# A gated cross-attention block on one core: value products in two visits of six tiles instead of three of four, and the work around them re-timed

## The chip, the cores and the metric

The kernel runs on one core of a Trainium2 chip. The metric is the device time of one execution in microseconds (us). Three executions of the kernel before took 1373.48, 1373.49 and 1373.64 us; the median is 1373.49 us.

## The reference

For 32 batches, a layer norm of x (100 x 256) attends with 16 heads of 16 channels to a context of 1444 tokens, and a gated feed-forward part with quantized weights follows. Shortened:

```
x (32, 100, 256); ctx (32, 1444, 256); mask (32, 1444)
q = layernorm(x) @ Wq.T + bq;  k = ctx @ Wk.T + bk;  v = ctx @ Wv.T + bv      # 16 heads x 16
probs = softmax(clip(where(mask, clip(q k^T / 4, -50, 50), -10000), -50, 50))
delta = clip(residual_scale, 0, 0.3) * ((probs @ v) @ Wo.T + bo)
x = x + tanh(g_xattn) * (layernorm(delta) * gamma + beta)
n = activation_quant(layernorm(x))                       # 127 / max|row|, rounded
h = silu(n @ weight_quant(w1).T) * (n @ weight_quant(w2).T)      # hidden 704
x = x + tanh(g_ffn) * (activation_quant(h) @ weight_quant(w3).T)
```

## The kernel before

All matmuls run transposed: tokens of the context lie on partitions. The 1444 tokens of a batch are 12 tiles of 121 (the last has 113), and three chunks of four tiles. A batch `b` is a loop of 12 steps `n = 0..11`, and each engine has its own written-out program of these steps; only semaphores tie the programs together. `c` is the next batch, `d` the one before.

In step n TensorE (PE) does, in this order: `scores(b, n, 0)` (L1196: four matmuls for one half of the head pairs), half of a context item, a piece of a neighbour batch's small work, the value products if the step has them ("a visit"), `scores(b, n, 1)`, and the other half of the context item. ScalarE (ACT) takes each score half through an exponential into one of `NE` buffers `e_sb`, VectorE (DVE) clips the whole tile (`clip`, L787, 121 x 1600), and a visit (`attend`, `pv`, L1216) multiplies `VISIT` clipped tiles with the values into one PSUM bank; each tile waits for its own clip, and is 32 matmul records. In the kernel before the visits are in steps 1, 5 and 9, over the four tiles up to n - LAG = n - 2.

A context item `w` of 12 makes keys or values: chunk u = w // 4 has two key items (L1237, 484 columns each) and two value items (L1251). Item w runs in step w + ITEM, so with ITEM = 4 the items 8 to 11 of a batch run in steps 0 to 3 of that batch itself, the others in steps 4 to 11 of the batch before. Around an item: `split_head` and `split_rest` (DVE, L748 and L754, in steps 1/2, 5, 9) turn a loaded chunk into a high and a low part, and `split_head` of a chunk must wait until the last value item of the chunk two before it (`pe_ctx`) has read the same buffer; `k_rest` (DVE, L778) makes the low part of the keys.

Then SP issues the stacking: `stack_k` is 12 DMAs (L305) that lay a chunk's keys into one of two `k_st` buffers, after the keys are there and after the second score half of the last tile of the chunk that held the buffer. The stack of c's chunk 0 waits for `scores(b, 7, 1)` and is awaited by `scores(c, 0, 0)`; chunk 1 runs from step 11 to step 4, chunk 2 from step 3 to step 8. `stack_q` is 12 DMAs issued by GpSimd (POOL, L476) for the queries, in its step 8, after `q_rest` (DVE, L833, step 6).

The small work: attention output of d (DVE `attention_read` L848 in step 1, `attention_out` step 2; PE `delta` L1284 in step 3; DVE `delta_out` L873 in step 3), x of d for the feed-forward (DVE step 5), `x_turn` L1268, `x_query` L1275 (PE steps 4 and 5), `x2_turn` L1290 (7), gate and up products `up` L1302 (8 to 10), then `h_max`, `h_scale`, `h_round`, `h_quant` on DVE, `h_turn` L1309 (PE, step 1 of the batch after) and `down` L1315 (step 2). `x_turn` waits for `delta_out`. A second, guarded pass over all batches exists in the program (the branches with `base`) and runs only if non-finite values were seen.

## Time and profile before

| | us |
|---|---|
| median of three executions | 1373.49 |
| the profiled execution | 1372.54 |
| its span, first to last instruction | 1370.8 |
| PE busy / DVE busy / ACT busy / POOL busy | 1310.4 / 1124.0 / 961.6 / 457.0 |
| one batch in the middle (613.33 to 653.33) | 40.0 |

The span has a set-up of some 55 us in which the weights are prepared, 32 batches, and a tail from about 1335 us in which the last batch's small work runs alone. A busy share is an average over all of these. Matmuls overlap, so the distance from one start to the next is what one costs, and the printed duration of a single one is longer than that.

### The profile page before, as it was taken

What the parts mean: (1) busy time and instruction counts of PE and PEld (TensorE: products, weight loads), DVE (VectorE), ACT (ScalarE), POOL (GpSimd) and SP (SyncE); (2) the same over time, 40 slices, a digit from 0 to 9 for tenths busy, and PEclk for the clock granted to TensorE, in tenths of its full rate; (3) what the DMA queues carried; (4) which work ended last, traced back from release to release, by engine and by line L of the source; (5) the groups of instructions that cost most, each with busy time, mean ns of one, the idle gap of its engine ahead of it and who ended that gap; (6) DMA issues with size and microseconds to landing.
All of it is one profiled execution on the core that took longest, in us unless ns stands there. A gap on an engine that the chain in (4) does not pass through costs nothing.

```text
span 1370.8 us, 48003 instructions
## 1 busy us (share of the span) xinstructions
PE 1310.4 (96%) x19984; PEld 1211.7 (88%) x19984; DVE 1124.0 (82%) x2241; ACT 961.6 (70%) x1602; POOL 457.0 (33%) x760
## 2 busy tenths in 40 slices
PE   5599999999999999999999999999999999999982
PEld 4599999999999999999999999999999999999971
DVE  5668888888888888888888888888888888888864
ACT  2367777777777777777777777777777777777761
POOL 3623332333332233333223333423333332333310
PEclk9699999999999999999999999999999999999995
DMA  7467667767776776776677677767777776777620
GB/s 213 104 164 175 166 162 170 174 161 184 175 163 160 176 165 161 187 178 161 165 179 170 157 191 170 167 161 168 167 170 184 168 167 166 171 171 168 152 62 8
DMA packets 142477, 222.12 MB, mean 162 GB/s; under 512 B 29162, under 2 KB 135598, under 8 KB 142254
## 3 DMA queue, kind: packets, MB, share of 16 engines
q1 hardware_dynamic: 129966, 199.31, 60.5%
q0 software_dynamic: 12288, 19.69, 6.7%
q8 instruction: 159, 2.61, 0.9%
q14 instruction: 64, 0.52, 0.1%
HBM read 54.00 MB, written 3.28 MB: 42 GB/s over the span
## 4 chain that ended last, share of the span: by engine, by line
PE 87%; SPq 4%; DVE 3%; DMA 2%; POOL 2%; ACT 1%; issue 1%; DVEq 0%; POOLq 0%; ACTq 0%
PE sc L1196 22%; PE pvb L1216 19%; PE cb L1251 18%; PE cb L1237 17%; SPq L305 4%; PE mb L1302 3%; PE mb L1275 2%; PE mb L1284 2%; DMA k_st<-k_lo 2%; PE mb L1315 2%; PE mb L1309 1%; POOL q_st L476 0%; PE mb L1268 0%; ACT e_sb L554 0%; POOL e_sb L514 0%
## 5 line engine op out<-in xcount | busy, mean ns | idle before, releaser
L554 ACT ACTIVATE e_sb<-sc 121x800 f32<-121x800 f32 (+1 forms) x768 | 645.9, 847 | 150.9 <-PE sc L1196 138.5
L1196 PE MATMUL sc<-q_st,k_st 96*121 96x200 f32 (+1 forms) x3072 | 476.2, 278 | 9.5 <-DMA q_st<-bd_hi 4.1
L1196 PEld LDWEIGHTS sc<-q_st,k_st 96*121 96x121 f32 (+1 forms) x3072 | 415.1, 187 | 38.2 <-issue 10.9
L787 DVE TENSOR_SCALAR e_sb<-e_sb,hi_b 121x1600 f32<-121x1600 f32 (+1 forms) x384 | 400.2, 1049 | 5.9 <-ACT e_sb L554 5.9
L1216 PE MATMUL pvb<-e_sb,v_sb 121*32 121x100 f32 x12288 | 286.4, 251 | 0.0
L1216 PEld LDWEIGHTS pvb<-e_sb,v_sb 121*32 121x32 f32 x12288 | 265.1, 110 | 22.3 <-issue 19.2
L1251 PE MATMUL cb<-wv_hi,c_hi 128*121 128x256 f32 (+1 forms) x768 | 222.3, 289 | 9.9 <-DVE k_lo L778 9.7
L778 DVE SCALAR_TENSOR_TENSOR k_lo<-cb,bk_c,k_hi 128x484 fp32r<-128x484 f32 (+1 forms) x192 | 134.4, 701 | 110.5 <-ACT k_hi L566 110.5
L1251 PE MATMUL cb<-wv_hi,c_lo 128*121 128x256 f32 (+1 forms) x768 | 216.3, 282 | 0.0
L1251 PE MATMUL cb<-wv_lo,c_hi 128*121 128x256 f32 (+1 forms) x768 | 216.2, 282 | 0.0
L476 POOL DMA_DIRECT2D q_st<-bd_hi x256 | 164.6, 647 | 115.9 <-DVE bd_lo L833 113.1
L447 POOL TENSOR_SCALAR d_ve<-dmv,scal 100x1 f32<-100x1 f32 x32 | 43.9, 1373 | 433.4 <-DVE dmv L883 433.4
L1237 PE MATMUL cb<-c_hi,wk_hi 128*128 128x484 f32 (+1 forms) x384 | 154.5, 402 | 0.0
L1251 PEld LDWEIGHTS cb<-wv_hi,c_hi 128*121 128x121 f32 (+1 forms) x768 | 142.2, 185 | 11.2 <-DVE k_lo L778 10.4
L1237 PE MATMUL cb<-c_lo,wk_hi 128*128 128x484 f32 (+1 forms) x384 | 147.1, 383 | 0.0
L1237 PE MATMUL cb<-c_hi,wk_lo 128*128 128x484 f32 (+1 forms) x384 | 147.1, 383 | 0.0
L1251 PEld LDWEIGHTS cb<-wv_hi,c_lo 128*121 128x121 f32 (+1 forms) x768 | 141.3, 184 | 0.1
L1251 PEld LDWEIGHTS cb<-wv_lo,c_hi 128*121 128x121 f32 (+1 forms) x768 | 140.4, 183 | 0.0
L566 ACT ACTIVATE k_hi<-cb,bk_c 128x484 fp32r<-128x484 f32 (+1 forms) x192 | 127.4, 664 | 4.8 <-PE cb L1237 4.8
L754 DVE TENSOR_TENSOR c_lo<-c_in,c_hi 128x968 fp32r<-128x968 f32 (+1 forms) x96 | 112.5, 1172 | 0.0
L575 ACT ACTIVATE v_sb<-cb 121x512 f32<-121x512 f32 x160 | 97.1, 607 | 21.0 <-PE cb L1251 21.0
L476 POOL DMA_DIRECT2D q_st<-bd_lo x128 | 91.3, 713 | 0.1
(139 smaller groups left out, 1529.5 us busy)
## 6 DMA issues: line engine op xcount, KB each, us to landing
k_st<-k_hi SPq DMA_DIRECT2D x512, 121.0 KB, 2.8
c_in<-in_ctxT SPq DMA_DIRECT2D x64, 484.0 KB, 3.9
k_st<-k_lo SPq DMA_DIRECT2D x256, 121.0 KB, 3.0
k_st<-k_hi SPq DMA_DIRECT2D x256, 119.0 KB, 3.4
c_in<-in_ctxT SPq DMA_DIRECT2D x32, 476.0 KB, 4.7
k_st<-k_lo SPq DMA_DIRECT2D x128, 119.0 KB, 3.1
q_st<-bd_hi POOLq DMA_DIRECT2D x256, 50.0 KB, 3.3
q_st<-bd_lo POOLq DMA_DIRECT2D x128, 50.0 KB, 3.3
```

Source lines behind the costliest of these rows:

```text
L305: sp.dma_start(k_st[st_slot(b, u)][QR * part:QR * (part + 1), :, j, 0:CL[u]].bitcast(f32), src[slot][QR * j:QR * (j + 1), :, 0:CL[u]].bitc ...
L476: nc.gpsimd.dma_start(q_st[b.par][QR * part:QR * (part + 1), :, j, :].bitcast(f32), src[QR * j:QR * (j + 1), :, :, :].rearrange("p k a s - ...
L554: nc.scalar.activation(e_sb[e_slot(b, n)][0:TL[n], k * SW:(k + 1) * SW].rearrange("p (o c) -> p o c", o=2), sc[q % NSC][0:TL[n], :, 0:2 * PW],
L566: nc.scalar.activation(k_hi[slot][:, o, 0:CL[u]], cb[o][:, 0:CL[u]], ACT.Identity, bias=bk_c[:, o:o + 1]).then_inc(k_hi_done, 1)
L575: nc.scalar.activation(v_sb[0:TL[n], n:n + 2, :, 0:4:3, :].rearrange("p n q a d -> p (n q) a d"), cb[i][0:TL[n], :].rearrange("p (q a d) - ...
L754: V.tensor_tensor(c_lo[slot][:, :, 0:w], c_in[slot][:, :, 0:w], c_hi[slot][:, :, 0:w].bitcast(f32), ALU.subtract).then_inc(split_done, 1)
L778: V.scalar_tensor_tensor(k_lo[slot][:, o, 0:w], cb[o][:, 0:w], bk_c[:, o:o + 1], k_hi[slot][:, o, 0:w].bitcast(f32), ALU.add, ALU.subtract ...
L787: V.tensor_scalar(e, e, E_LO, hi_b[b.par][0:TL[n], n:n + 1], ALU.max, ALU.min).then_inc(clip_done, 1)
L1196: last = T_.matmul(sc[q % NSC][0:TL[n], e // 2, (e % 2) * PW:(e % 2 + 1) * PW], k_st[st_slot(b, n // TPC)][:, pr // NQ, pr % NQ, t0:t0 + T ...
L1216: last = T_.matmul(pvb[QR * j:QR * (j + 1), col:col + S], v_sb[0:TL[n], n, pr, 2 * a:2 * a + 2, :].rearrange("p x d -> p (x d)"), e[0:TL[n ...
L1237: last = T_.matmul(cb[o][:, 0:w], wt[:, k, o * P:(o + 1) * P], ct[slot][:, k, 0:w], start=i == 0, stop=i == 5)
L1251: last = T_.matmul(cb[i][0:TL[n], half * H:(half + 1) * H], ct[slot][:, k, t0:t0 + TL[n]], wt[:, k, :], start=(k == 0 and a == 0), stop=(k ...
```

## The change

`VISIT` goes from 4 to 6 and `LAG` from 2 to 1: the visits are in steps 0 (tiles 6 to 11 of d) and 6 (tiles 0 to 5 of b). `NE` goes from 6 to 7 exponential buffers; the room comes from the guard's scratch tiles, which now lie in the seventh buffer (the guarded pass uses six), and two memsets of them leave the set-up. `ITEM` goes from 4 to 5: every context item, with its ACT and DVE parts, is one step later. The four gate and up products stand one each in PE steps 8, 9, 10 and 11, all ahead of the second score half; the ACT and DVE parts follow, so that `hidden_up(d, 1)` and `h_max` move from DVE's steps 10 and 11 into step 0 of the next batch.

```diff
-    NE = 6
-    VISIT = 4
+    NE = 7
+    NEG = 6
+    VISIT = 6
-    LAG = 2
-    ITEM = 4
+    LAG = 1
+    ITEM = 5
...
+        care = [e_sb[NE - 1][:, i * H:(i + 1) * H] for i in range(6)]
...
         def e_slot(b, n):
-            return (NT * b.par + n) % NE
+            return (NT * b.par + n) % NEG if b.base else (NT * b.n + n) % NE
...
-            nc.gpsimd.memset(big_pos[:, :], INF_TO)
-            nc.gpsimd.memset(big_neg[:, :], -INF_TO)
...
-                    if prev and n in (9, 10):
-                        ffn_up(d, n - 9)
-                    if prev and n in (8, 9):
-                        ffn_gate(d, n - 8)
+                    if prev and n in (8, 10):
+                        ffn_gate(d, (n - 8) // 2)
+                    if prev and n in (9, 11):
+                        ffn_up(d, (n - 8) // 2)
...
-                        if n in (9, 10):
-                            hidden_gate(d, n - 9)
+                        if n in (9, 11):
+                            hidden_gate(d, (n - 9) // 2)
...
                     if prev2 and n == 0:
-                        for step in (h_scale, h_round, h_quant):
+                        hidden_up(b.plus(-2), 1)
+                        for step in (h_max, h_scale, h_round, h_quant):
                             step(b.plus(-2))
...
-                        if n in (9, 10):
-                            hidden_up(d, n - 9)
-                        if n == 11:
-                            h_max(d)
+                        if n == 10:
+                            hidden_up(d, 0)
...
-                    has_pv = n % VISIT == 1 and (n > VISIT or prev)
+                    has_pv = n % VISIT == 0 and (n >= VISIT or prev)
...
-                        if n == 8:
-                            up(d, 0, 0)
-                        if n in (9, 10):
-                            up(d, n - 9, 1)
+                        if n >= 8:
+                            up(d, (n - 8) // 2, n % 2)
                     attend()
                     if prev2 and n == 1:
                         h_turn(b.plus(-2))
-                    if prev and n == 9:
-                        up(d, 1, 0)
```

How the instructions stand in three places. The first is VectorE in steps 0 and 1 of a steady batch, from the clip of the last tile (113 partitions) to the first read of the attention sums (`oT<-pvb`). Before:

```order
L787 TENSOR_SCALAR e_sb<-e_sb,hi_b 113x1600 [waits exp_done]
L943 TENSOR_SCALAR tiny<-tiny 100x1 [waits dve_post]
L945 RECIPROCAL tiny<-tiny 100x1 [waits dve_post]
L949 TENSOR_SCALAR th<-gs,tiny 100x704 [waits dve_post]
L953 TENSOR_SCALAR hq<-th 100x704 [waits dve_post]
L954 TENSOR_SCALAR tiny<-tiny,k_y 100x1
L748 CAST c_hi<-c_in 128x968 [waits pe_ctx,c_loaded1]
L778 SCALAR_TENSOR_TENSOR k_lo,watch<-cb,bk_c,k_hi 128x476 [waits k_hi_done]
L787 TENSOR_SCALAR e_sb<-e_sb,hi_b 121x1600 [waits pool_x,exp_done]
L848 TENSOR_SCALAR oT<-pvb,submask 128x200 [waits pv_done]
```
After:

```order
L788 TENSOR_SCALAR e_sb<-e_sb,hi_b 113x1600 [waits exp_done]
L936 TENSOR_TENSOR gs<-th,us 100x352 [waits dve_post,act_post]
L940 TENSOR_REDUCE tiny<-gs 100x1 [waits dve_post]
L944 TENSOR_SCALAR tiny<-tiny 100x1 [waits dve_post]
L946 RECIPROCAL tiny<-tiny 100x1 [waits dve_post]
L950 TENSOR_SCALAR th<-gs,tiny 100x704 [waits dve_post]
L954 TENSOR_SCALAR hq<-th 100x704 [waits dve_post]
L955 TENSOR_SCALAR tiny<-tiny,k_y 100x1
L749 CAST c_hi<-c_in 128x968 [waits pe_ctx,c_loaded1]
L788 TENSOR_SCALAR e_sb<-e_sb,hi_b 121x1600 [waits pool_x,exp_done]
L849 TENSOR_SCALAR oT<-pvb,submask 128x200 [waits pv_done]
```
Behind the clip stand two more operations (`gs`, the reduce to `tiny`); the key part `k_lo` that stood between the cast of the next chunk (`c_hi<-c_in`, chunk 0 of c) and the clip has gone to a later step. The cast waits for `pe_ctx`: it needs item 7 of the batch, which before ran in step 11 of the batch ahead and now runs in step 0, its second half behind the visit.

The second place is TensorE in steps 5 and 6, from the query product (`mb<-xnT,wq`) on. Before, the visit follows it at once:

```order
L1275 MATMUL mb<-xnT,wq 128x100 [waits act_x]
L1275 MATMUL mb<-xnT,wq 128x100 x3
L1216 MATMUL pvb<-e_sb,v_sb 32x100 [waits dve_post,v_done,clip_done]
L1216 MATMUL pvb<-e_sb,v_sb 32x100 x15
L1216 MATMUL pvb<-e_sb,v_sb 32x100 [waits clip_done]
L1216 MATMUL pvb<-e_sb,v_sb 32x100 x15
```
After, from the same product's second row on, the visit (`pvb`) comes one step later, in step 6, behind two score halves and two key halves (`cb`):

```order
L1277 MATMUL mb<-xnT,wq 128x100 x3
L1198 MATMUL sc<-q_st,k_st 121x200 [waits exp_done]
L1198 MATMUL sc<-q_st,k_st 121x200 x3
L1239 MATMUL cb<-c_hi,wk_hi 128x484
L1239 MATMUL cb<-c_lo,wk_hi 128x484
L1239 MATMUL cb<-c_hi,wk_lo 128x484
L1198 MATMUL sc<-q_st,k_st 121x200 [waits exp_done]
L1198 MATMUL sc<-q_st,k_st 121x200 x3
L1239 MATMUL cb<-c_hi,wk_hi 128x484 [waits v_done]
L1239 MATMUL cb<-c_lo,wk_hi 128x484
L1239 MATMUL cb<-c_hi,wk_lo 128x484
L1218 MATMUL pvb<-e_sb,v_sb 32x100 [waits dve_post,v_done,clip_done]
```
It now takes tiles 0 to 5, and the sixth of them waits for the clip that VectorE does in this same step 6.

The third place is TensorE in step 9, between the score half that frees a stacking buffer (step 7) and the one that needs it (step 0 of the next batch). Before:

```order
L1237 MATMUL cb<-c_hi,wk_hi 128x484 [waits v_done]
L1237 MATMUL cb<-c_lo,wk_hi 128x484
L1237 MATMUL cb<-c_hi,wk_lo 128x484
L1302 MATMUL mb<-w12q,x2T 100x352 [waits act_post]
L1302 MATMUL mb<-w12q,x2T 100x352
L1216 MATMUL pvb<-e_sb,v_sb 32x100 [waits v_done,clip_done]
L1216 MATMUL pvb<-e_sb,v_sb 32x100 x15
L1216 MATMUL pvb<-e_sb,v_sb 32x100 [waits clip_done]
L1216 MATMUL pvb<-e_sb,v_sb 32x100 x15
L1216 MATMUL pvb<-e_sb,v_sb 32x100 [waits v_done,clip_done]
```
After:

```order
L1239 MATMUL cb<-c_hi,wk_hi 128x484 [waits v_done]
L1239 MATMUL cb<-c_lo,wk_hi 128x484
L1239 MATMUL cb<-c_hi,wk_lo 128x484
L1304 MATMUL mb<-w12q,x2T 100x352 [waits act_post]
L1304 MATMUL mb<-w12q,x2T 100x352
L1198 MATMUL sc<-q_st,k_st 121x200 [waits exp_done]
L1198 MATMUL sc<-q_st,k_st 121x200 x3
L1239 MATMUL cb<-c_hi,wk_hi 128x484
L1239 MATMUL cb<-c_lo,wk_hi 128x484
L1239 MATMUL cb<-c_hi,wk_lo 128x484
```
The visit that stood here, four tiles, is gone; no value product is left between steps 7 and 0.

## Rows read from the trace of the kernel before

**Rows 1.** The page: busy time by engine, and TensorE clock in 40 slices.
```profile
PE 1310.4 (96%) x19984; PEld 1211.7 (88%) x19984; DVE 1124.0 (82%) x2241; ACT 961.6 (70%) x1602; POOL 457.0 (33%) x760
...
PEclk9699999999999999999999999999999999999995
```

**Rows 2.** TensorE waits of the whole span: engine line waited for, total, times, longest.
```profile
PE sc L1196 <- DMA k_st<-k_lo: 2.0, 6, 0.7
```

**Rows 3.** TensorE timeline: start, us, instruction, shapes, count.
```profile
603.79 0.46 PE L1302 MATMUL mb<-w12q,x2T 128*100 128x352 bf16 x2
604.18 2.97 PE L1216 MATMUL pvb<-e_sb,v_sb 121*32 121x100 f32 x128
607.08 0.50 PE L1302 MATMUL mb<-w12q,x2T 128*100 128x352 bf16 x2
...
619.55 0.44 PE L1309 MATMUL mb<-identb,hq 100*128 100x100 bf16 x6
...
631.44 2.96 PE L1216 MATMUL pvb<-e_sb,v_sb 121*32 121x100 f32 x128
...
639.04 0.65 PE L1196 MATMUL sc<-q_st,k_st 96*121 96x200 f32 x4
...
653.33 0.47 PE L1196 MATMUL sc<-q_st,k_st 96*121 96x200 f32 x3
```

**Rows 4.** Chain of waits, same stretch: start, us, and what ran.
```profile
607.58 0.41 PE sc L1196 x4
607.99 0.68 PE cb L1237 x3
```

**Rows 5.** VectorE timeline, same batch.
```profile
613.61 0.88 DVE L939 TENSOR_REDUCE tiny<-gs 100x1 f32<-100x704 f32 x1
...
616.93 0.66 DVE L748 CAST c_hi<-c_in 128x968 fp32r<-128x968 f32 x1
...
619.69 0.42 DVE L848 TENSOR_SCALAR oT<-pvb,submask 128x200 f32<-128x200 f32 x1 [0.50 <-PE pvb L1216]
...
631.01 0.48 DVE L893 SCALAR_TENSOR_TENSOR x<-dn,d_r,x_res 100x256 f32<-100x256 f32 x1 [1.07 <-POOL d_r L452]
...
638.27 1.05 DVE L787 TENSOR_SCALAR e_sb<-e_sb,hi_b 121x1600 f32<-121x1600 f32 x1
639.23 0.57 DVE L833 SCALAR_TENSOR_TENSOR bd_lo<-bd,bd_hi 128x400 fp32r<-128x400 f32 x1
...
647.84 0.53 DVE L935 TENSOR_TENSOR gs<-th,us 100x352 f32<-100x352 f32 x1
```

**Rows 6.** Issues of the stacking copies: timelines of the SP queue and of GpSimd.
```profile
627.31 1.23 SPq L305 DMA_DIRECT2D k_st<-k_hi  x2
...
635.64 0.60 SPq L305 DMA_DIRECT2D k_st<-k_lo  x1
...
639.77 1.93 SPq L305 DMA_DIRECT2D k_st<-k_hi  x2
...
650.51 0.61 SPq L305 DMA_DIRECT2D k_st<-k_lo  x1
...
799.72 1.23 SPq L305 DMA_DIRECT2D k_st<-k_hi  x2
...
808.93 1.02 SPq L305 DMA_DIRECT2D k_st<-k_lo  x1
...
640.45 1.40 POOL L476 DMA_DIRECT2D q_st<-bd_hi  x1 [2.97 <-DVE bd_lo L833]
...
647.87 0.54 POOL L476 DMA_DIRECT2D q_st<-bd_hi  x1
```

**Rows 7.** Stretches of the last batch: width, busy PE to POOL, clock, DMA share, GB/s.
```profile
1318.00:1319.00 1.00, 0.34 (x5) 0.17 (x3) 1.00 (x2) 1.00 (x3) 1.00 (x1) 1.00 0.47 109
1320.00:1321.00 1.00, 1.00 (x7) 1.00 (x6) 0.39 (x1) 1.00 (x3) 0.00 (x0) 0.50 0.00 0
1322.00:1323.00 1.00, 1.00 (x22) 0.76 (x24) 0.90 (x1) 1.00 (x3) 0.00 (x0) 0.50 0.00 0
```

More of the change, by code:

```diff
@@ L101, in flamingo_block @@
     INF_TO = 10000.0
-    assert 2 * NT % NE == 0 and (STEPS * NT) % NSC == 0 and NB % 2 == 0 and NB >= 8
+    assert 2 * NT % NEG == 0 and NEG < NE and NT % VISIT == 0 and (STEPS * NT) % NSC == 0 and NB % 2 == 0 and NB >= 8
     assert all(c % 2 == 0 for c in CL) and STEPS * SW == EW
@@ L137, in flamingo_block @@
         odd, odd_sum = sb("odd", [P, 1]), sb("odd_sum", [P, 1], i32)
-        big_pos, big_neg = sb("big_pos", [P, H]), sb("big_neg", [P, H])
-        g_pos, g_k = sb("g_pos", [P, H]), sb("g_k", [P, H])
-        g_gt, g_lt = sb("g_gt", [P, H], i32), sb("g_lt", [P, H], i32)
         x_in = [sb(f"x_in{i}", [S, H]) for i in range(2)]
@@ L162, in flamingo_block @@
         e_sb = [sb(f"e_sb{i}", [P, EW]) for i in range(NE)]
+        care = [e_sb[NE - 1][:, i * H:(i + 1) * H] for i in range(6)]
+        big_pos, big_neg, g_pos, g_k = care[0:4]
+        g_gt, g_lt = care[4].bitcast(i32), care[5].bitcast(i32)
         zt, oT = sb("zt", [P, KT, S]), sb("oT", [P, KT, S])
@@ L202, in flamingo_block @@
         stored = sem("stored")
-        odd_known = sem("odd_known")
+        odd_known, care_known = sem("odd_known"), sem("care_known")
         care_c, care_k, care_v = sem("care_c"), sem("care_k"), sem("care_v")
@@ L519, in passes @@
                 if base:
+                    nc.gpsimd.memset(big_pos, INF_TO)
+                    nc.gpsimd.memset(big_neg, -INF_TO).then_inc(care_known, 1)
                     x_rstd_of(whole(0, base))
@@ L552, in exps @@
                 if k == 0 and not (isinstance(b.n, int) and b.n == 0 and n < NE):
-                    act.wait_ge(pv_done, TILE.after(b, n) - NE)
+                    act.wait_ge(pv_done, TILE.after(b, n) - (NEG if b.base else NE))
                 nc.scalar.activation(e_sb[e_slot(b, n)][0:TL[n], k * SW:(k + 1) * SW].rearrange("p (o c) -> p o c", o=2),
@@ L1111, in passes @@
                 if base:
+                    dve.wait_ge(care_known, 1)
                     b = whole(0, base)
@@ L1142, in passes @@
                 clip(e, NT - 1)
-                for step in (h_scale, h_round, h_quant, result):
+                hidden_up(e.plus(-1), 1)
+                for step in (h_max, h_scale, h_round, h_quant, result):
                     step(e.plus(-1))
```

## The prediction

> **What bounds the kernel now.** I read the page first: TensorE is busy for 96% of the span, VectorE for 82%, ScalarE for 70%, and TensorE's clock is full but for the set-up and the tail [rows 1]. In the list of TensorE's waits nothing of the 32 batches matters; the one to remember is small, six waits of 2.0 us together, for the stacking DMAs of the keys [rows 2]. So a batch takes 40 us because TensorE has 40 us of matmuls, and no matmul goes away in this change. It can gain only at the borders between kinds of matmul, and lose by waits that are now just hidden. So I read TensorE's timeline of one batch for the distances [rows 3, 4], and VectorE's and SP's timelines of the same batch for how early the things that it needs are ready [rows 5, 6].
>
> **The visits themselves.** A visit of four tiles takes 2.90 us (604.18 to 607.08), 0.725 a tile [rows 3]; six tiles take 4.35. One visit less per batch saves its border: the gate product's two matmuls start 0.39 us before the visit [rows 3], some 0.2 more than two such matmuls need, and a score half behind a visit takes about 0.1 more than the 0.41 of rows 4. Against that, the gate and up products, of which two lay at a visit, now stand between a context half and a score half four times, at about 0.1 each. I count 0 (bounds -0.3 and +0.2 a batch).
>
> **First wait: the clip of tile 5, in step 6.** With LAG at 1, the visit in step 6 needs the clip that VectorE does in step 6; before, that clip was wanted only in step 9. What sets VectorE's time is a second edit: with ITEM at 5, the last value item of chunk 1 runs in step 0, its second half behind the visit, and the cast of the next chunk at the head of VectorE's step 1 waits for it. Before, that cast began at 616.93, 2.6 us before TensorE had finished its visit of step 1 (619.55) [rows 3, 5]. Now VectorE is through with step 0 early and then stands until step 0 of TensorE has ended; behind the cast are queued, in order, the clip of tile 0, the attention sums, the key parts, three clips and the whole chain to the feed-forward's input.
>
> From the end of TensorE's step 0, VectorE needs: the cast 0.66, a clip 0.96 (638.27 to 639.23), then everything from the attention read to the end of clip 5, 619.69 to 639.23 = 19.54 [rows 5]. Three key parts lie in that stretch in both kernels. Sum 21.2, and 0.14 for the hand-over (619.69 against 619.55) [rows 3, 5], at both ends: 21.4.
>
> TensorE needs, until it reaches tile 5: a score half and a key half, 0.41 + 0.68 [rows 4]; from the transposes of step 1 to the end of the query product 619.55 to 631.44 = 11.89 [rows 3]; then two score halves and two key halves, 2.2; about 0.1 to enter the visit; five tiles, 3.6. Sum 18.9. It waits 21.4 - 18.9 = 2.5; I take 2.4, since the cast overlaps the next operation a little. (A part of it will show earlier, at `x_turn` in step 4, which waits for `delta_out` of VectorE's step 3; that is the same lateness, not more.) Bounds: 1.3, if VectorE's pause of 1.07 for GpSimd inside the 19.54 [rows 5] vanishes; 3.1, if a key part has to wait for ScalarE. 30 batches of 2.4: 72 us.
>
> **Second wait: the stack of chunk 0, in step 0.** The 12 DMAs of the next batch's chunk 0 can start when `scores(b, 7, 1)` is done, and `scores(c, 0, 0)` wants them. Before, the distance on TensorE was 639.04 to 653.33 = 14.3 us, with the visit of step 9 in it [rows 3]. Without that visit it is 14.3 - 2.9 - 0.2 = 11.2. The other two chunks gain what this one loses, a visit now lies in each of their stretches and is longer.
> The stack needs: 0.73 until SP starts (639.77), then to the last issue 10.74 in this batch, 9.21 in another (799.72 to 808.93), and 8.33 for chunk 2 (627.31 to 635.64), when GpSimd issues nothing [rows 6]; then the landing, under 2.82, since TensorE went on at 653.33 without a wait [rows 3]. GpSimd's 12 query DMAs take 640.45 to 648.4 and began 0.7 us after the stack [rows 6]; now they begin some 2.5 before it, as they hang on step 6's clip, so about two thirds of them still lie beside it. I take 9.1 to the last issue and 2.7 to land: 0.73 + 9.1 + 2.7 = 12.5, a wait of 1.3. Bounds: 0.73 + 8.33 + 2.3 - 11.2, about 0.2 (the 2.3 is my estimate for a landing half a microsecond under its bound), and 0.73 + 10.74 + 2.82 - 11.2 = 3.1. I stay at the typical batch, as rows 2 show that the 10.74 is near the worst. 31 batch starts of 1.3: 40 us.
> The Trainium skill ("DMA: Bandwidth & Descriptors", Issuing engines are not separate DMA queues) says that DMAs issued by different engines run on the same 16 DMA engines and interleave. Rows 6 agree (10.74 beside GpSimd's, 8.33 without). By that rule alone the two thirds of an overlap would put the last issue at 9.9 and the wait at 2.2, 27 us more in all, inside the bounds.
>
> The two waits add up: the first delays `scores(b, 7, 1)`, from which the second is counted, and the second delays step 0, whose end starts VectorE's 21.4 us again.
>
> **TensorE's clock.** In the last batch, where TensorE had work for 0.34 of the microsecond 1318 to 1319, its clock was at half from 1320 on, and still at 1322 to 1323 [rows 7]. A wait of 1.5 to 2.4 us in one piece may do the same. Some 3 us at half speed cost 1.5; behind the step 6 wait half of it is swallowed by the second wait. I count it in every other batch: 30 x 0.4 = 12 us (bounds 0 and 45).
>
> **The rest.** `hidden_up` and `h_max` (0.53 and 0.88 [rows 5]) move into VectorE's step 0, where it stands idle for the cast anyway, so they are covered; `h_turn` in step 1 wants the result over 7 us after step 0 begins. In the tail they are bare, 1.4 us, and the last visit has two tiles more, 1.45: 3 us. Batch 0 has one context item less and the last batch one more: 0. The seventh buffer has no price: step 6's exponentials write it before the visit frees tile 0's. Without it ScalarE would stand. Two memsets fewer in a set-up that waits for weights: 0. In steps 8 to 11 ScalarE has no visit to catch up in; its two exponentials, an item and a gate stay just under TensorE's step, cover thin, and if gone, a few tenths a batch.
>
> Sum: 72 + 40 + 12 + 3 = 127 on the profiled execution's 1372.5 gives 1499.5; the median of the runs is 0.95 above that execution, so 1500 us.
>
> **Rivals.** (1) *Only the clip wait.* The stack of chunk 0 gets through in the shorter stretch, because the DMA load spreads over a longer batch. For it: 8.33 without GpSimd. Against: even then nothing is left over. 1373.5 + 72 + 12 + 3 = 1460.
> (2) *All at the upper bounds*, with the clock falling each time: 30 x 3.1 + 31 x 3.1 + 45 + 3 = 237, 1611 us. For it: rows 6's slow stack, rows 7. Against: only six small waits in the kernel before.
> (3) *Both waits about half as long*, since I mis-add the lateness of an engine that has 18% of idle time [rows 1]: 1373.5 + 60 = 1433.
> (4) *Faster.* VectorE is done with clip 5 in time and the stack lands in time; then a batch has one visit border less, 0.3 us, 31 times: 1364 us. It decides at 2.4 us on VectorE's path: if the cast of chunk 0 began where it did before, 2.6 us ahead of the visit's end, this case would hold. The waits of the code speak against it: the cast waits for the value item now in step 0.
> The Trainium skill ("TensorEngine Tiling (Array Packing)", Key Properties) says that changing the tiling mode drains the engine; the visits use another mode (32 output rows) than their neighbours. The 0.39 us before the visit agrees; by that rule the change gains this rival's 0.3 us per batch and nothing else.
>
> **Chances.** Forecast 0.57, with its own range 1455 to 1550; (1) 0.15; (2) 0.13, mostly its lower part, 1550 to 1611; (3) 0.10; (4) 0.05. Runs of this kernel tell apart about 0.2%, 2.7 us. Slower by over 0.2%: (1), (2), (3) and the forecast, 0.95; case (4) is split, within 0.2% 0.02 (the border of a visit worth nothing), faster 0.03. The range 1420 to 1565 holds the forecast, (1) and (3) and the foot of (2), about 0.83.
>
> **What the profile after would show.** The first wait: TensorE standing in front of the last 32 value matmuls of step 6's visit, waiting for VectorE's clip, or at `x_turn` for `delta_out`, together some 2.4 us a batch, and VectorE idle before the cast by about 2.5 us with `cb`'s value item as releaser. The second: TensorE's step 0 waiting for `k_st` by some 1.3 us, 31 times. A batch would take 43.6 to 44 us, and TensorE's clock would show slices under full. The forecast is wrong if VectorE is not idle before that cast, or if clip 5 ends before TensorE is through with tile 4, or if step 0 starts without a wait for the stack.

## The result and the profile after

| | kernel before | changed kernel |
|---|---|---|
| median of the runs | 1373.49 us (1371.28 to 1373.64, 4 runs) | 1491.47 us (1483.22 to 1494.61, 4 runs) |
| profiled execution, span | 1372.54 us, 1370.8 us | 1489.05 us, 1487.2 us |
| mean granted clock of TensorE | 0.975 | 0.964 |

The change makes the kernel slower: ratio 1.085, 95% interval 1.081 to 1.090. The profiled execution took 116.5 us more. Line numbers of the changed kernel differ from those before by one or two (the scores are L1198, the visits L1218, the value items L1253, the clip L788, the cast L749).

The page after, first the busy times, then the clock; it answers to [rows 1].

```profile
PE 1353.5 (91%) x19984; PEld 1235.1 (83%) x19984; DVE 1140.1 (77%) x2241; ACT 959.4 (65%) x1602; POOL 511.4 (34%) x758
...
PEclk9699999999999999999999999999999999999995
```

The instructions of TensorE are as many as before; its share fell from 96 to 91%. The 40 slices of the clock hide what a batch does, as will be seen. The chain of work that ended last, by engine, shows who took over: VectorE, with 3% of it before and 37% after. First the kernel before, then the changed one:

```profile
PE 87%; SPq 4%; DVE 3%; DMA 2%; POOL 2%; ACT 1%; issue 1%; DVEq 0%; POOLq 0%; ACTq 0%
```

```profile
PE 45%; DVE 37%; POOL 6%; issue 6%; SPq 3%; DMA 2%; ACT 1%; DVEq 0%; POOLq 0%; ACTq 0%
```
 The waits say more (engine and line, what it waited for, us in total, times, longest); it is the same view as [rows 2], in which six waits for `k_st` made 2.0 us.

```profile
PE pvb L1218 <- DVE e_sb L788: 50.7, 31, 2.2
...
PE mb L1270 <- DVE dl L874: 12.6, 30, 0.4
...
PE pvb L1218 <- issue: 7.2, 12, 1.1
...
PE sc L1198 <- DMA k_st<-k_lo: 4.2, 6, 1.2
```

The first two are new, and each comes about once a batch: the last 32 matmuls of step 6's visit wait for the clip of tile 5, and `x_turn` in step 4 waits for `delta_out`. The third is new and was not forecast: "issue" is time in which TensorE waits for nothing that the profile shows, here inside a visit (the last section says what it is). The fourth, the forecast's second wait, is hardly there.

TensorE's timeline of one batch (start, us, instruction, what it waited for), against [rows 3]:

```profile
644.71 0.90 PE L1218 MATMUL pvb<-e_sb,v_sb 121*32 121x100 f32 x32 [1.68 <-DVE e_sb L788]
...
647.94 0.65 PE L1198 MATMUL sc<-q_st,k_st 96*121 96x200 f32 x4
...
659.27 0.67 PE L1198 MATMUL sc<-q_st,k_st 96*121 96x200 f32 x4
...
660.59 4.35 PE L1218 MATMUL pvb<-e_sb,v_sb 121*32 121x100 f32 x192
...
676.67 0.36 PE L1270 MATMUL mb<-identf,xn 100*128 100x100 f32 x2 [0.43 <-DVE dl L874]
...
682.27 3.63 PE L1218 MATMUL pvb<-e_sb,v_sb 121*32 121x100 f32 x155
...
686.30 0.37 PE L1218 MATMUL pvb<-e_sb,v_sb 121*32 121x100 f32 x5 [0.41 <-issue]
...
687.58 0.90 PE L1218 MATMUL pvb<-e_sb,v_sb 121*32 121x100 f32 x32 [0.91 <-DVE e_sb L788]
```

Read 647.94 as `scores(b, 7, 1)` and 659.27 as `scores(c, 0, 0)`: the stretch in which the stack of chunk 0 must land is 11.33 us, 11.2 by the forecast, and no wait stands at its end. The six tiles of a visit take 4.28 us from its start to the next instruction's (660.59 to 664.87), 4.35 by the forecast. At 686.30 the visit stops for 0.41 us with nothing to wait for, and the wait for the clip behind it is shorter (0.91 us).

VectorE in the same batch, against [rows 5]:

```profile
666.37 0.67 DVE L749 CAST c_hi<-c_in 128x968 fp32r<-128x968 f32 x1 [1.70 <-PE cb L1253]
666.95 1.05 DVE L788 TENSOR_SCALAR e_sb<-e_sb,hi_b 121x1600 f32<-121x1600 f32 x1
667.91 0.42 DVE L849 TENSOR_SCALAR oT<-pvb,submask 128x200 f32<-128x200 f32 x1
...
679.86 0.48 DVE L894 SCALAR_TENSOR_TENSOR x<-dn,d_r,x_res 100x256 f32<-100x256 f32 x1 [1.06 <-POOL d_r L451]
...
686.47 1.05 DVE L788 TENSOR_SCALAR e_sb<-e_sb,hi_b 121x1600 f32<-121x1600 f32 x1
```

VectorE stands 1.70 us for the value item of step 0, as the forecast wanted it, and from the attention read to the end of clip 5 (686.47 + 0.97) it needs 19.5 us, the forecast's 19.54. The pause of 1.06 us for GpSimd is part of that in both kernels; no run here took it away by itself.

Last the SP queue, the 12 copies of chunk 0 in that stretch, against [rows 6]:

```profile
648.67 1.23 SPq L306 DMA_DIRECT2D k_st<-k_hi  x2
...
656.81 0.60 SPq L306 DMA_DIRECT2D k_st<-k_lo  x1
```

8.14 us from first to last issue here. Over 28 batches the median of this distance is 7.45 us (9.1 in the forecast, 9.2 in the kernel before); from the first issue to the end of the last it is 8.0 us, with 10.2 in the kernel before. GpSimd's copies of the queries, first and last, in the same stretch:

```profile
645.79 0.64 POOL L475 DMA_DIRECT2D q_st<-bd_hi  x1 [2.97 <-DVE bd_lo L834]
...
652.82 1.40 POOL L475 DMA_DIRECT2D q_st<-bd_hi  x1
```

They begin 2.88 us before the stack. Before, they began 0.7 us after it [rows 6].

From one `h_turn` to the next, 29 batches of the kernel before take 40.1 us in the mean (39.97 at least); those of the changed one take 44.1, and 42.71 at least. In 14 of the 29 the mean clock of the batch is 0.96, and eight of these take 44.25 to 44.30. One batch of the changed kernel with the clock full and one without (width; busy PE, PEld, DVE, ACT, POOL; clock; DMA share; GB/s):

```profile
538.65:581.37 42.72, 40.61 (x625) 37.41 (x625) 34.57 (x70) 29.70 (x51) 16.12 (x23) 1.00 0.63 152
753.31:797.57 44.26, 42.17 (x626) 38.80 (x625) 34.89 (x70) 30.03 (x51) 14.41 (x23) 0.96 0.61 149
```

They differ by 1.54 us and by the clock, and the same instructions of TensorE are busy 1.56 us longer. In windows of 2 us the second batch shows where (width, busy PE, clock, DMA share, GB/s):

```profile
773.00:775.00 2.00, 1.30 (x36) 1.00 0.06 17
775.00:777.00 2.00, 2.00 (x9) 0.52 0.23 51
777.00:779.00 2.00, 2.00 (x15) 0.63 0.44 103
779.00:781.00 2.00, 2.00 (x20) 1.00 0.47 100
```

The clip wait (1.65 us there) ends at 773.7, and from about 775 the granted clock is at its lower level, 1.2 GHz, for 3.4 us.

### The profile page after: what moved, and what is told of

It reads as the page before. It is cut to its first block, busy times and chain, and to the rows that moved or that the text cites. A ratio compares the mean times of both kernels' runs of the same rounds, so it can differ in the third digit from the quotient of the medians.

```text
span 1487.2 us, 48000 instructions
## 1 busy us (share of the span) xinstructions
PE 1353.5 (91%) x19984; PEld 1235.1 (83%) x19984; DVE 1140.1 (77%) x2241; ACT 959.4 (65%) x1602; POOL 511.4 (34%) x758
## 4 chain that ended last, share of the span: by engine, by line
PE 45%; DVE 37%; POOL 6%; issue 6%; SPq 3%; DMA 2%; ACT 1%; DVEq 0%; POOLq 0%; ACTq 0%
PE sc L1198 12%; PE pvb L1218 11%; PE cb L1253 11%; DVE e_sb L788 10%; PE cb L1239 7%; DVE c_lo L755 4%; DVE k_lo L779 3%; DVE zt L860 3%; POOL d_ve L446 3%; SPq L306 3%; PE mb L1304 2%; DVE c_hi L749 1%; DMA k_st<-k_lo 1%; POOL d_rstd L449 1%; DVE x L894 1%
## 5 line engine op out<-in xcount | busy, mean ns | idle before, releaser
L555 ACT ACTIVATE e_sb<-sc 121x800 f32<-121x800 f32 (+1 forms) x768 | 661.9, 863 | 392.7 <-PE sc L1198 386.7
L1198 PE MATMUL sc<-q_st,k_st 96*121 96x200 f32 (+1 forms) x3072 | 492.4, 284 | 11.2 <-DMA k_st<-k_lo 4.2
L1198 PEld LDWEIGHTS sc<-q_st,k_st 96*121 96x121 f32 (+1 forms) x3072 | 420.5, 189 | 46.2 <-issue 15.2
L788 DVE TENSOR_SCALAR e_sb<-e_sb,hi_b 121x1600 f32<-121x1600 f32 (+1 forms) x384 | 400.5, 1050 | 30.8 <-ACT e_sb L555 28.7
L1218 PE MATMUL pvb<-e_sb,v_sb 121*32 121x100 f32 x12288 | 289.1, 250 | 58.0 <-DVE e_sb L788 50.7
L1218 PEld LDWEIGHTS pvb<-e_sb,v_sb 121*32 121x32 f32 x12288 | 264.9, 110 | 82.8 <-DVE e_sb L788 57.6
L1253 PE MATMUL cb<-wv_hi,c_hi 128*121 128x256 f32 (+1 forms) x768 | 231.6, 302 | 9.9 <-DVE k_lo L779 9.8
L475 POOL DMA_DIRECT2D q_st<-bd_hi x256 | 187.2, 735 | 113.4 <-DVE bd_lo L834 108.6
L1253 PE MATMUL cb<-wv_hi,c_lo 128*121 128x256 f32 (+1 forms) x768 | 220.9, 288 | 0.0
L1253 PE MATMUL cb<-wv_lo,c_hi 128*121 128x256 f32 (+1 forms) x768 | 220.1, 287 | 0.0
L1253 PEld LDWEIGHTS cb<-wv_hi,c_hi 128*121 128x121 f32 (+1 forms) x768 | 146.2, 190 | 17.3 <-DVE k_lo L779 10.8
L749 DVE CAST c_hi<-c_in 128x968 fp32r<-128x968 f32 (+1 forms) x96 | 69.1, 719 | 110.3 <-PE cb L1253 110.3
L1253 PEld LDWEIGHTS cb<-wv_hi,c_lo 128*121 128x121 f32 (+1 forms) x768 | 145.8, 190 | 0.1
L1253 PEld LDWEIGHTS cb<-wv_lo,c_hi 128*121 128x121 f32 (+1 forms) x768 | 144.9, 189 | 0.0
L567 ACT ACTIVATE k_hi<-cb,bk_c 128x484 fp32r<-128x484 f32 (+1 forms) x192 | 131.9, 687 | 9.6 <-PE cb L1239 9.5
```

The costliest lines, as they stand in the source:

```text
L475: nc.gpsimd.dma_start(q_st[b.par][QR * part:QR * (part + 1), :, j, :].bitcast(f32), src[QR * j:QR * (j + 1), :, :, :].rearrange("p k a s - ...
L555: nc.scalar.activation(e_sb[e_slot(b, n)][0:TL[n], k * SW:(k + 1) * SW].rearrange("p (o c) -> p o c", o=2), sc[q % NSC][0:TL[n], :, 0:2 * PW],
L567: nc.scalar.activation(k_hi[slot][:, o, 0:CL[u]], cb[o][:, 0:CL[u]], ACT.Identity, bias=bk_c[:, o:o + 1]).then_inc(k_hi_done, 1)
L788: V.tensor_scalar(e, e, E_LO, hi_b[b.par][0:TL[n], n:n + 1], ALU.max, ALU.min).then_inc(clip_done, 1)
L1198: last = T_.matmul(sc[q % NSC][0:TL[n], e // 2, (e % 2) * PW:(e % 2 + 1) * PW], k_st[st_slot(b, n // TPC)][:, pr // NQ, pr % NQ, t0:t0 + T ...
L1218: last = T_.matmul(pvb[QR * j:QR * (j + 1), col:col + S], v_sb[0:TL[n], n, pr, 2 * a:2 * a + 2, :].rearrange("p x d -> p (x d)"), e[0:TL[n ...
```

## The experiments

Each ratio is to the kernel before in the same session (its medians were 1370.9, 1371.9, 1372.2 and 1371.3 us), with its 95% interval.

**Context items back at four** (changed kernel).

```diff
-    ITEM = 5
+    ITEM = 4
```

> The changed kernel with ITEM back at 4, so that the cast of chunk 0 on VectorE no longer waits for a value item behind the visit of step 0. Theory A (the one in the prediction: that cast is what makes clip 5 late): the wait in step 6 goes, 1.7 us plus the refill of TensorE's pipeline, and with it the half-clock stretches; about 2.7 us a batch and 22 us of clock less, so 1385 to 1400 us. Theory B (the chain on VectorE hangs on the clip of tile 0, whose exponential waits for a score half behind the same visit; the cast only hides 0.5 us of that): the chain starts 0.5 to 0.6 us earlier at most, the wait in step 6 falls from 1.7 to about 1.1 to 1.2, and the time from 1491 to about 1470, to 1450 if the clock stays up. In both, VectorE's idle time before the cast (110 us in all) falls to a few us, and under B most of it reappears as a wait of clip 0 for ScalarE.

Measured: 1508.46 us, ratio 1.101 (1.099 to 1.103), which neither theory has. TensorE's waits:

```profile
PE cb L1253 <- DVE k_lo L779: 70.1, 92, 8.6
PE pvb L1218 <- DVE e_sb L788: 34.1, 31, 1.3
```

With the cast free to start early, the clip is still waited for, 1.1 us each time where it was 1.6. Even these 0.5 us don't say that VectorE is earlier: the value items now wait for the low part of the keys (60 us beyond the 10 that the changed kernel's list has too), so TensorE comes to the visit later itself. From `h_turn` to the end of the clip wait it takes 21.1 us in a batch of this run and 20.4 (753.31 to 773.70) in the changed kernel. So the cast's wait is not what makes clip 5 late, or not alone; its own share is not separated, since a key part stands ahead of the clip again. With these visits the later items are a repair, not the fault.

**Visits one step later, clip lag back at two** (changed kernel: six tiles, steps 1 and 7).

```diff
-    LAG = 1
+    LAG = 2
-                    has_pv = n % VISIT == 0 and (n >= VISIT or prev)
+                    has_pv = n % VISIT == 1 and (n > VISIT or prev)
```

> The changed kernel with LAG back at 2: visits of six tiles in steps 1 and 7. Clip 5 is wanted a step later, and the visit no longer stands in front of the exponential of tile 0. Theory A/B (LAG 1 with the visit in step 0 is the cause of the clip wait): no clip wait, no x_turn wait, full clock, about 40.1 us a batch: 1370 to 1382 us. Rival (the size of the visit, six tiles, is what VectorE cannot serve): a wait of a microsecond or more stays in step 7, 1400 us or more. For the second wait of the prediction: the stretch for the stack of chunk 0 stays 11.2 us; if it is short after all, TensorE waits for k_st in many batches, up to 1.3 us each (then 1400 to 1415).

Measured: 1521.79 us, ratio 1.110 (1.108 to 1.111), mean clock 0.936. The first row is of ScalarE, the second of TensorE:

```profile
ACT e_sb L555 <- PE pvb L1218: 143.6, 32, 5.5
```

```profile
PE cb L1253 <- DVE k_lo L779: 70.2, 34, 8.3
```

Both theories miss: no clip is waited for, and yet the time is the longest of all. ScalarE's exponential of tile 7 waits up to 5.5 us for tile 0's buffer, and the rest follows it. Six tiles in a visit and a lag of two need more than seven buffers; the lag of one is what makes the large visit possible, and it is the lag that costs.

**The lag alone** (kernel before, four-tile visits in steps 0, 4 and 8, items and buffers as they were).

```diff
-    LAG = 2
+    LAG = 1
-                    has_pv = n % VISIT == 1 and (n > VISIT or prev)
+                    has_pv = n % VISIT == 0 and (n >= VISIT or prev)
```

> The kernel before with LAG 1 alone: visits of four tiles in steps 0, 4 and 8. If LAG 1 by itself were the cause, TensorE would wait for VectorE's clips in steps 4 and 8 and lose 1 to 2 us a batch (1400 to 1440 us). By the rows of the kernel before clip 3 would be done about when the visit of step 4 comes to its fourth tile, so under the theory that it takes the six tiles together with LAG 1 (the visit wants clip 5 less than two visits after step 0), this one stays within 0.5% of 1373 us.

Measured: 1470.54 us, ratio 1.071 (1.069 to 1.074), where my theory said within 0.5% of 1373. One edit brings a loss nearly as large as the whole change's, but by other waits than the changed kernel's.

```profile
PE cb L1251 <- DVE k_lo L778: 28.3, 34, 9.4
PE mb L1302 <- ACT us L627: 21.3, 32, 1.4
PE pvb L1216 <- issue: 14.1, 7, 3.0
```

ScalarE has become the late one. By my reading of the order, the visit of step 5 used to cover its four activations behind `x_query`, and now that visit is in step 4. That is not shown. A batch takes 42.64 us at least, 2.7 more than before. The recorded waits give 1.2 of that. The rest lies in wider distances between the starts of TensorE's instructions, of which the list shows nothing; I did not separate them.

**The feed-forward's input behind clip 5** (changed kernel: `x1_norm` to `x2_quant`, six small operations, in VectorE's step 6).

```diff
-                        if n == 5:
+                        if n == 6:
                             x1_norm(d)
...
```

> The changed kernel with one thing moved on VectorE: the six operations that make the feed-forward input (x1_norm to x2_quant, 1.9 us) stand in step 6 behind clip 5 and q_rest instead of in step 5 ahead of them. No work is taken away. If the wait in step 6 is lateness of VectorE's queue, it shrinks by 1.9 us, to nothing or 0.2, and the half-clock stretches that followed it vanish with it; the 0.4 us wait at x_turn stays. Then a batch takes about 40.7 to 41, and the kernel 1395 to 1410 us. If the wait came from elsewhere (the exponential of tile 5, the value item), nothing changes: 1491 us. A side effect: with the wait gone the stack of chunk 0 has less time beside GpSimd's DMAs; if the second wait of the prediction is real in that state, waits for k_st of up to 1.3 us a batch appear.

Measured: 1451.11 us, ratio 1.059 (1.058 to 1.061), mean clock 0.978.

```profile
PE sc L1198 <- DMA k_st<-k_lo: 27.1, 28, 2.3
...
PE mb L1270 <- DVE dl L874: 12.6, 30, 0.4
PE pvb L1218 <- issue: 11.7, 18, 1.6
```

The clip wait is gone, and with it the clock's loss. So it was VectorE's queue ahead of clip 5. But the gain was 40 us where 81 to 96 were expected: the second wait, absent before, is now there, 28 times. The stack of chunk 0 takes 9.3 us (median, first issue to end of the last) in place of 8.0: GpSimd's copies now begin 1.5 us before it, and 9 of the 12 are issued beside it.

**`delta_out` ahead of clip 2** (the kernel above, and this).

```diff
+                        if n == 3:
+                            delta_out(d)
...
                         if n == 3:
-                            delta_out(d)
                             delta_stats(d)
```

> The changed kernel with the feed-forward's input later on VectorE (as in the run before: 1451 us) and delta_out ahead of the clip of tile 2 in VectorE's step 3. Theory Q (each remaining wait of TensorE on VectorE is the place of that instruction in VectorE's queue): x_turn's wait for delta_out (12.6 us, 30 times 0.4) goes, the clip of tile 2 has 3 steps in hand, and nothing else gets later: 1451 - 13 = 1438 us, and the wait for the stack of chunk 0 stays at 27 us. Rival R (VectorE is late as a whole): the 0.4 comes back in front of the visit of step 6 or in front of the stack, 1451 us.

Measured: 1443.87 us, ratio 1.053 (1.050 to 1.056). `x_turn` waits no more (12.6 us); a clip wait of 7.8 us, 26 times up to 0.7, takes part of it back, and the stack's stays at 28.7. Half of each theory: the queue place was the cause, and VectorE is still close behind.

**Without the queries' copies** (the kernel above; from batch 2 on `stack_q` issues nothing and its waits are constants, so this kernel leaves out the queries of all later batches and serves for its time alone).

```diff
+                if not b.base and b.n >= 2:
+                    return
                 for j in range(NQ):
...
```

> The same kernel as e5_x2late_dl, but from batch 2 on GpSimd's 12 DMAs of the queries (stack_q) are left out; the queries of the batches 0 and 1 are used again. Theory C (the second wait is contention: SP's 12 DMAs take 9.8 us beside GpSimd's and under 8 without): the stack of chunk 0 gets done some 2 us earlier, the wait for k_st (27 us) goes, with the half clock behind it: 1438 - 27 - 8 = 1403 us. Rival D (the stack starts too late and SP's own issuing sets its length): it still takes over 9 us, k_st is waited for as before, 1435 us.

Measured: 1404.65 us, ratio 1.025 (1.023 to 1.027). `k_st` waits:

```profile
PE sc L1201 <- DMA k_st<-k_lo: 1.6, 2, 1.2
```

The forecast of theory C to within 2 us. The stack of chunk 0 shrinks from 9.2 to 8.3 us in the median; those 0.9 us a batch are the wait (28.7 us in 30 times). Of the 39 us that the time fell, this wait is 27 (28.7 to 1.6) and fewer stops at the visits are 5 ("issue", 10.6 to 5.6 in the lists); the other 7 I can't place. The second wait is contention between GpSimd's copies and SP's.

**One part alone: the four products** (kernel before, the products as in the diff, `hidden_up(1)` and `h_max` in VectorE's step 0).

> The kernel before with one part of the change alone: a step for each gate or up product (and hidden_up(1) and h_max in VectorE's step 0). Theory (this part costs nothing while VectorE idles in step 0 for the cast, and two borders more cost 0.1 us each): 1371 to 1378 us. Rival (h_turn in step 1 gets hq too late, since three operations more stand before it): 30 times 0.5 or more, 1386 us and up, with waits at h_turn for DVE.

Measured: 1384.52 us, ratio 1.010 (1.009 to 1.012). Neither expectation: 12.7 us, and no wait of a batch in the list. Against a batch of before, one of 40.08 us loses 0.17 and 0.12 in the steps that got a product and gains 0.21 at the visit that lost two. Others, of 40.41, lose 0.14 at `x_turn` and 0.26 at `x2_turn` besides. I take that for VectorE's lateness in pieces too short for the list; it is not shown.

**One part alone: the items** (kernel before with `ITEM` at 5).

> The kernel before with one part of the change alone: the context items one step later. Theory B (the clip of tile 5 alone made the first wait; the later cast costs only what nobody waits for, as LAG is 2): 1371 to 1376 us, with VectorE idle before the cast in step 1. Rival A (a cast held up by the value item makes VectorE late for all that follows, the point of the prediction): waits at x_turn or at the visits of 0.5 us a batch and more, 1386 us and up.

Measured: 1386.86 us, ratio 1.012 (1.010 to 1.014). This time rival A has it, at its lower end (the wait at `x_turn` is 0.24 us a batch, half of what it said):

```profile
PE mb L1268 <- DVE dl L873: 7.1, 30, 0.4
```

Nearly every batch takes 40.4 us instead of 40.0, with `x_turn` waiting. With a lag of two no clip is late, but `delta_out` is.

**The queries' copies earlier** (the kernel of 1443.87, nothing left out).

```diff
...
+                    if n == 5 and nxt:
+                        stack_q_parts(b.plus(1), "hi", (0, 2))
                     if n == 5 and prev:
                         ffn_factors(b.plus(-1))
                     if n == 8 and nxt:
-                        stack_q(b.plus(1))
+                        stack_q_parts(b.plus(1), "lo", (1,))
```

> The same as e5_x2late_dl (1444 us), but with nothing left out: GpSimd issues the eight DMAs of the queries' high part as soon as q_head is done (before ffn_factors), and only the four of the low part where all twelve stood. They then lie beside the first 2 to 3 us of the stack of chunk 0 instead of beside 7 of its 9.8 us. Theory C (contention lengthens the stack; without the queries' DMAs 1405 us): the wait for k_st falls from 28.7 us to under 10, 1410 to 1420 us. Rival (it is the number of DMAs per batch, or the chunk's own start, and not what lies beside it): the wait stays above 20 us, 1435 to 1445 us; or ffn_factors, now behind eight DMAs on GpSimd, makes ScalarE's gate late and takes the place, with waits at h_turn or up, also about 1440.

Measured: 1419.42 us, ratio 1.034 (1.032 to 1.036). As theory C has it; this is a kernel that computes everything.

```profile
PE pvb L1226 <- DVE e_sb L795: 8.0, 27, 0.7
PE pvb L1226 <- issue: 7.7, 16, 0.8
PE sc L1206 <- DMA k_st<-k_lo: 7.5, 12, 1.5
```

**Two low halves later** (that kernel; `split_rest` of chunk 0 from VectorE's step 2 into step 3, of chunk 1 from step 5 into step 7).

> The same as e9_q_early with two more operations moved on VectorE: the low half of chunk 0 (split_rest, 1.16 us) from step 2 behind delta_gamma in step 3, where VectorE stood 1.07 us for GpSimd, and that of chunk 1 from step 5 to step 7. Theory (what is left of the first wait, at delta, x_turn and the visit of step 6, 0.7 us a batch, is VectorE's queue): 0.7 x 30 = 21 us less than e9_q_early, 1390 to 1400 us. Rival (what is left is the six-tile visit itself and its neighbours, or the supply of instructions): within 5 us of e9_q_early. Neither forecasts less than the kernel before.

Measured: 1506.85 us, ratio 1.097 (1.095 to 1.100): 87 us slower than the kernel it was to improve. TensorE's and SP's waits:

```profile
PE sc L1209 <- DMA k_st<-k_lo: 71.8, 51, 3.8
```

```profile
SPq L292 <- DVE c_lo L762: 479.8, 61, 15.1
```

I had looked at VectorE and TensorE and forgotten SP: its loads of the context wait for just these low halves, and the stacks of the keys are queued behind the loads.

**SP's order** (that kernel; each stack ahead of the load that waits for a low half).

```diff
-                if nxt:
-                    sp.wait_ge(split_done, SPLIT.after(b.plus(1), "lo0"))
-                    load_c(b.plus(1), 2)
                 if prev2:
                     store(b.plus(-2))
                 stack_k(b, 2)
+                if nxt:
+                    sp.wait_ge(split_done, SPLIT.after(b.plus(1), "lo0"))
+                    load_c(b.plus(1), 2)
+                if nxt:
+                    stack_k(b.plus(1), 0)
                 if nxt2:
                     sp.wait_ge(split_done, SPLIT.after(b.plus(1), "lo1"))
                     load_c(b.plus(2), 0)
-                if nxt:
-                    stack_k(b.plus(1), 0)
```

> e10_q_early_split came out at 1507 us and not at 1390 to 1400. Its waits: TensorE for k_st 71.8 us, 51 times, and SP's loads of the context for c_lo 480 us (194 in the changed kernel). Theory S (SP works in order, and each load waits there for a low half that I had made later, with a stack of the keys queued behind it): the same kernel with SP's order changed, so that the stack of chunk 2 stands ahead of the load that waits for the low half of chunk 0, and the next stack of chunk 0 ahead of the load that waits for that of chunk 1. The waits for k_st fall to those of e9_q_early (7.5 us) or under, the clip wait of e9 (8.0 us) stays gone: 1390 to 1405 us. Rival (VectorE's new order itself is what makes the stacks late, through the key parts behind the moved halves): k_st is waited for as in e10, over 1480 us. Rival L (the loads now start late and lie beside the stack of chunk 1, which is then waited for, or the cast is): 1420 to 1460 us.

Measured: 1422.66 us (1416.40 to 1431.18), ratio 1.038 (1.033 to 1.043).

```profile
PE pvb L1229 <- issue: 22.8, 22, 4.0
...
PE sc L1209 <- DMA k_st<-k_lo: 4.3, 8, 0.8
```

The cause of the 87 us is shown: the stacks are hardly waited for any more (4.3 us), nor is any clip. The time I gave for it was wrong, since something else took the place: the visits stop with "issue", 22 times and up to 4.0 us. One batch that escapes it shows what the arrangement is worth at best, the six-tile visits and the single products together (the columns as in the table of two batches above; first this kernel, then the kernel before):

```profile
1187.93:1227.78 39.85, 39.85 (x625) 37.27 (x625) 33.97 (x70) 29.54 (x51) 18.28 (x23) 1.00 0.69 168
```

```profile
659.55:699.53 39.98, 39.98 (x629) 37.29 (x625) 34.18 (x69) 29.87 (x50) 13.48 (x23) 1.00 0.73 175
```

0.13 us a batch, 4 us in all, from one batch.

**Six buffers for the exponentials** (changed kernel, in which ScalarE waits as if there were six).

```diff
-                    act.wait_ge(pv_done, TILE.after(b, n) - (NEG if b.base else NE))
+                    act.wait_ge(pv_done, TILE.after(b, n) - NEG)
```

> The changed kernel, in which ScalarE waits before each exponential as if there were six buffers and not seven. Theory of the prediction (without the seventh, ScalarE stands in steps 6 and 0 until the visit has freed tile 0 of it): a wait of ScalarE of 1 to 2 us twice a batch; in step 6 TensorE waits in the visit anyway, so what is added is what ScalarE can't catch up, 0.3 to 1 us a visit: 1491 + 20 to 60 = 1510 to 1550 us. Rival (VectorE's clip is the later one in step 6, and ScalarE has 35% idle): no more than 1491 + 5 us.

Measured: 1485.77 us (1478.10 to 1488.63), not slower than the changed kernel's 1491.47. ScalarE does stand, and nobody waits for it:

```profile
ACT e_sb L555 <- PE pvb L1218: 50.7, 63, 2.8
```

No version here beats the kernel before.

## Why the prediction was right, and where it was not

The forecast was 1500 us in a range of 1420 to 1565, slower with 0.95. The time came out at 1491.5 us. The total is nearer than its terms are:

| term | forecast, us | found, us | from |
|---|---|---|---|
| first wait | 72 | 79 | 29 times 42.72 less 39.98 (2.1 of the 2.7 recorded as waits, the rest in wider distances between starts) |
| second wait | 40 | 2 | 4.2 against 2.0 in the lists |
| clock | 12 | 22 | about 14 batches of 29 longer by 1.55 |
| start and tail | 3 | 3 | the stretches outside the 29 batches |
| stops inside visits | 0 | 7 | 7.2 in the list (1.1 of it in step 6, where the clip wait is shorter for it) |
| not placed | 0 | 3 | what is left of 116.5 |

*The first wait* was right in place, size and count, and in its sum (19.5 us of VectorE's queue). Its named cause was at most a part. The prediction said that the held-up cast sets VectorE's time, and in its rival (4) that if the cast began where it did before, the case for faster would hold. With the items back at four, clip 5 was no earlier and still waited for; the items alone cost the kernel before 15 us. What sets the wait is the whole queue ahead of clip 5: with six operations moved behind the clip it vanished.

*The second wait* is the term that was mis-sized: 40 us against 2. By the prediction's own sign, a step 0 that starts without a wait for the stack, this half of the mechanism was wrong. The step that failed is the 9.1 us to the last issue; it took 7.45, and 0.73 + 7.45 + 2.7 = 10.9 us fit into the 11.3. I let two thirds of GpSimd's copies lie beside the stack, begun 2.5 us before it. They begin 2.9 us before it in batches with the clock full and 4.4 in those where it fell, and 3 to 6 of the 12 are issued beside it: the first wait and the lower clock hold back `scores(b, 7, 1)` and with it the stack, and not GpSimd's copies. I also priced the copies beside it too high: with the items back at four, 8 of them lie beside the stack, and it takes 7.6 us to the last issue. The prediction added the two waits up; in truth the first pays for most of the second. Take the first away (copies 1.5 us ahead, 8.6 us to the last issue) and the second appears at 27.1 us (bounds 0.2 to 3.1 a batch, found 0.9), take GpSimd's copies away too and it is gone. So the wait was real, and whether it counted depended on the other. The Trainium skill ("DMA: Bandwidth & Descriptors", Issuing engines are not separate DMA queues) says that DMAs started by different engines run on the same 16 DMA engines and interleave. The runs agree: 1443.9 us with the copies of both engines side by side, 1404.7 without GpSimd's.

*The clock* was counted for every other batch, as it came, but at about 0.75 us each (0.4 over all) where it cost 1.55. I had let the second wait swallow half of it, and there was none.

*The borders* at 0 were right: -0.13 us in the one undisturbed batch. The Trainium skill ("TensorEngine Tiling (Array Packing)", Key Properties) says that changing the tiling mode drains the engine. That one batch agrees in sign with fewer changes being a gain; it shows less than half of the 0.3 us that I had taken from the rows.

*Covered at nothing* was wrong where it was said lightly. The products and `hidden_up` cost 12.7 us alone in the kernel before. There VectorE has 18% of idle time but nothing in hand at `x_turn` and `x2_turn`. In the changed kernel I did not separate this part. *The seventh buffer* was right at no price. Without it ScalarE does stand, as the prediction said, but nobody waits for it, so the kernel didn't need it.

*Rivals.* Rival (1), with the clip wait and no second wait, is what the list of waits shows. Its 1460 is 31 us low: 7 for the first wait, 10 for the clock, 7 for the stops inside visits, 2 for the second wait, and a rest. The forecast's 1500 had a wait too many and the other terms too small, and these cancelled, which is luck: the good total is no sign of a good sum. (2) and (3) fell too, as the first wait came at its full size and the second hardly at all, and (4) fell with the first wait.

The parts don't add up: 12.7 and 15 us for two edits alone, 100 for the lag alone, and 118 for all. And the repairs in a row (40, 7 and 24 us, then none) brought 1491 down to 1419, each uncovering the next wait: clip, stack, stops inside visits. What stays open is the rest: the batches of the last kernel take 1.7 us more than the kernel before's in the mean, and the lists account for 1.0 of it.

## What to carry to other kernels

Adding the waits of two places is only right where the first one delays everything that the second depends on; list what it doesn't delay, above all copies that share the DMA engines, since those get ahead. An engine's idle share says nothing of its margin at one place: VectorE idled 18% of the time, and a cast held up by 1.0 us (32.1 us in 32 times, with the items alone moved) cost 0.4 us a batch. When an operation moves, look for its name in every engine's waits, the loading queue's first: two low halves moved by one and two steps cost 87 us through loads that stood ahead of the stacks.

## What the hardware did that I had not expected

*TensorE runs out of instructions in a visit.* "issue" in the list of waits: 7.2 us in the changed kernel, 14.1 with four-tile visits in other steps, 22.8 in the last kernel, and none at the visits of the kernel before. The place of the stop moves evenly. The changed kernel's timeline, one visit in each of three batches; the count behind the last `x` is how many matmuls of the visit are left:

```profile
357.81 0.89 PE L1218 MATMUL pvb<-e_sb,v_sb 113*32 113x100 f32 x31 [0.54 <-issue]
...
403.17 0.72 PE L1218 MATMUL pvb<-e_sb,v_sb 113*32 113x100 f32 x23 [0.64 <-issue]
...
447.30 0.54 PE L1218 MATMUL pvb<-e_sb,v_sb 113*32 113x100 f32 x14 [0.19 <-issue]
```

It steps by 8 or 9 a batch, so the stop sits at a fixed distance in TensorE's program and not at an event of the batch. The page has a DMA queue for instructions:

```profile
q8 instruction: 159, 2.61, 0.8%
```

159 packets of 16.4 KB are 5 a batch. By the trace's packet times, each of the changed kernel's 12 stops at a visit ends 1.3 to 1.6 us after such a packet has been moved (the one before 357.81 was moved from 355.17 to 356.42), and so do the 22 of the last kernel, within 1.2 to 1.7 us. With 5 packets a batch that is no accident: TensorE stops for the next piece of its program, which arrives late. The longest (4.0 us, before 307.78; its packet was moved from 305.08 to 306.35) lies in a stretch in which the DMA engines are busy for 0.86:

```profile
305.00:307.00 2.00, 0.00 (x0) 0.00 (x0) 0.00 (x0) 0.00 (x0) 0.00 (x0) 1.00 0.86 197
```

Why a packet comes late is open. Leaving out the queries' copies halved the stops (10.6 to 5.6 us), which speaks for the load on the DMA engines, but no run changed the supply by itself.

*Equal waits, unequal clocks.* A wait of 1.68 us (before 644.71) left the clock full; one of 1.65 (before 773.70) was followed by 3 us at half. I did not find what tells the two apart.
